# One Trainium2 core: self-attention's decay multiply and row maximum fused, FP4 rounding of FFN weights split between VectorE and GpSimd, masked queries made inside the loop

## The reference

```
x = x + cross_attention(layernorm(x), ctx)     # 16 heads of 64
x = x + self_attention(layernorm(x))           # 16 heads of 16, latent keys and values
x = x + ffn(layernorm(x))                      # FP4 rounded inputs and weights, width 704

# self_attention, for each batch and head
scores = q @ k_rec.T / sqrt(256)
scores = scores * decay                        # decay[i, j] = exp(-0.01 * |i - j|)
out    = softmax(scores) @ v_rec

# rounding of the last dimension in blocks of 16
scale = max(|block|) / 6;  q = nearest_fp4(block / scale) * scale
```

## Time and profile before

| | |
|---|---|
| median of 3 runs | 1395.5 us (1392.56 to 1398.28) |
| the profiled execution's own time | 1398.23 us |
| its span in the trace | 1396.5 us |
| mean granted clock of TensorE | 0.973 |
| PE busy | 1314.0 us (94%) |
| DVE busy | 1001.9 us (72%) |
| ACT busy | 870.6 us (62%) |
| POOL busy | 669.5 us (48%), none of it from 1200.4 us on |
| attention loop | first scores at 1219.58 us, last values end at 1320.03 us |

### The profile page before, as it was taken

The page is one execution under the profiler, slowest core; times in us unless marked ns, Lnnn a source line. Parts: engine busy times, 40 slices in busy tenths (PEclk is TensorE's granted clock), DMA queues, the critical chain, the costliest instruction groups (busy, mean ns, idle before and its releaser), DMA issues. The chain is left out here.

```text
span 1396.5 us, 24647 instructions
## 1 busy us (share of the span) xinstructions
PE 1314.0 (94%) x9280; PEld 1123.8 (80%) x9280; DVE 1001.9 (72%) x1382; ACT 870.6 (62%) x1704; POOL 669.5 (48%) x817
## 2 busy tenths in 40 slices
PE   5899999999999999999999999999999998689857
PEld 5788888888888888888888888888888887378734
DVE  3666678667876777678866886688668868489576
ACT  3667666666666766666666666666666666346511
POOL 5654755475546544565547554755475444000000
PEclk9999999999999999999999999999999999889878
DMA  4010000000000011100000000000000003000000
GB/s 128 16 38 13 16 1 9 8 16 1 9 9 31 1 39 31 39 31 1 9 17 8 1 9 8 16 1 9 9 1 1 1 8 99 0 1 1 1 0 15
DMA packets 24902, 22.95 MB, mean 16 GB/s; under 512 B 4433, under 2 KB 24529, under 8 KB 24785
## 3 DMA queue, kind: packets, MB, share of 16 engines
q1 hardware_dynamic: 24784, 21.38, 5.1%
HBM read 20.85 MB, written 0.52 MB: 15 GB/s over the span
## 5 line engine op out<-in xcount | busy, mean ns | idle before, releaser
L661 ACT ACTIVATE pT_hi<-psT 128x512 fp32r<-128x512 f32 x512 | 292.4, 601 | 238.2 <-PE psT L417 223.5
L752 DVE TENSOR_TENSOR pT_lo<-psT,pT_hi 128x512 fp32r<-128x512 f32 x512 | 330.3, 685 | 101.0 <-ACT pT_hi L661 100.5
L746 DVE TENSOR_REDUCE negm<-psS 128x1 f32<-128x1024 f32 x256 | 311.8, 1218 | 47.9 <-PE psS L407 47.9
L325 POOL TENSOR_TENSOR kT<-kraw,khi 64x512 fp32r<-64x512 f32 x252 | 324.8, 1289 | 0.0
L626 ACT ACTIVATE prob<-psS,negm 128x1024 f32<-128x1024 f32 x256 | 285.8, 1116 | 1.0 <-DVE negm L746 1.0
L319 POOL CAST khi<-kraw 128x512 fp32r<-128x512 f32 x126 | 76.9, 610 | 415.6 <-ACT kraw L636 414.2
L417 PE MATMUL psT<-ident,prob 128*128 128x128 f32 x2048 | 268.5, 274 | 2.1 <-DVE pT_lo L752 2.1
L433 PE MATMUL psO<-pT_hi,v 128*128 128x256 f32 x1024 | 267.5, 294 | 2.1 <-DVE pT_lo L752 1.8
L417 PEld LDWEIGHTS psT<-ident,prob 128*128 128x128 f32 x2048 | 233.2, 140 | 36.1 <-issue 10.3
L434 PE MATMUL psO<-pT_lo,v 128*128 128x256 f32 x1024 | 255.7, 282 | 0.0
L433 PEld LDWEIGHTS psO<-pT_hi,v 128*128 128x128 f32 x1024 | 195.4, 191 | 3.3 <-DVE pT_lo L752 3.1
(11 more groups left out here) (231 smaller groups left out, 1578.6 us busy)
## 6 DMA issues: line engine op xcount, KB each, us to landing
cst<-in_ctx_dram SPq DMA_DIRECT2D x12, 512.0 KB, 3.8
oT<-in_ctx_dram SPq DMA_DIRECT2D x4, 512.0 KB, 5.3
wraw<-in_L_xattn_Wk_dram SPq DMA_DIRECT2D x8, 256.0 KB, 2.7
wraw<-in_L_xattn_Wv_dram SPq DMA_DIRECT2D x8, 256.0 KB, 2.7
wraw<-in_L_xattn_Wq_dram SPq DMA_DIRECT2D x8, 256.0 KB, 2.7
wo<-in_L_xattn_Wo_dram SPq DMA_DIRECT2D x8, 256.0 KB, 2.7
ff_wdn<-in_L_ffn_w_down_dram SPq DMA_DIRECT2D x1, 704.0 KB, 7.5
ff_win<-in_L_ffn_w_gate_dram SPq DMA_DIRECT2D x1, 640.0 KB, 5.0
```

The lines of the kernel that those rows point to most:

```text
L325: pool.tensor_tensor(kT[half, m // 2 % KRING, h, 1, :], raw[own, :], khi[own, :].bitcast(F32), ALU.subtract).then_inc(k_split, 1)
L661: act.activation(pT_hi[:, i % PRING, :], psT[:, t % 2, :], ACT.Copy).then_inc(ph_ok, 1)
L746: dve.tensor_reduce(negm[:, g % 2, h, qt, c:c + 1], psS[:, qt, :], AX.X, ALU.max, negate=True)\
L752: dve.tensor_tensor(pT_lo[:, i % PRING, :], psT[:, t % 2, :], pT_hi[:, i % PRING, :].bitcast(F32), ALU.subtract).then_inc(pl_ok, 1)
```

## The change

1. The multiply and the maximum of a unit become two `tensor_tensor_reduce` of 128x256, one for each half, that write the product to `sa_s` and the row maximum to a new tile `sa_top`; a TENSOR_SCALAR of 128x2 then turns its sign into `negm`. PE's wait for the PSUM tile is on `top_ok`, behind the pair.
2. Operations 4, 7, 8 and 9 of each weight chunk move to POOL. The tiles `wa`, `wm`, `wamax` and `wrs` get two buffers. The six operations left on DVE stand behind a unit's sign turn: operation 0 at unit `CHUNK_AT[c]`, 1 to 3 one unit later, 5 and 6 three units later. DVE's operation 5 waits for POOL's operation 4; DVE's operation 0 of chunk c waits for POOL's last of chunk c - 2. `turn_w` is at iterations `CHUNK_AT[c]` + 8 and + 9.
3. The first 3 masked queries are made ahead of the loop, the other 13 one at a time behind the sign turn of units 0 to 12.
4. The tiles of the row rounding are slices of the weight tiles, and DVE waits for POOL's last weight operation before the LayerNorm of the FFN.

```diff
-    WPU = 2
+    CHUNK_AT = (0, 4, 9, 13, 18, 22)
...
+        top = tile("sa_top", [P, U, QT])
...
-        wa = tile("ff_wa", [P, WCH])
+        wa = tile("ff_wa", [P, 2, WCH])
...
+            for c in range(CHUNKS):
+                src = weight_rows(c)
...
+                a, m = wa[:, c % 2, 0:width], wm[:, c % 2, 0:width]
+                pool.wait_ge(wq, 6 * c + 4)
+                pool.tensor_tensor(blocks(a), blocks(src), wide(wrs), ALU.mult).then_inc(wp, 1)
+                pool.wait_ge(wq, 6 * c + 6)
+                pool.tensor_tensor(a, a, m, ALU.add).then_inc(wp, 1)
+                pool.wait_ge(wp, 4 * c + 2)
+                pool.tensor_tensor(a, a, m, ALU.subtract).then_inc(wp, 1)
+                pool.wait_ge(wp, 4 * c + 3)
+                pool.tensor_tensor(blocks(src), blocks(a), wide(wamax), ALU.mult).then_inc(wp, 1)
...
-                    pe.wait_ge(sd_done, u - 1)
+                    pe.wait_ge(top_ok, 2 * (u - 1))
...
-                pe.wait_ge(wq, quantized_at(c))
+                pe.wait_ge(wp, 4 * (c + 1))
...
-            for h in range(H):
+            def own_rows(h):
                 dve.wait_ge(proj_ok, at[("q", h // HPT)] + 1)
                 dve.tensor_scalar(qm[:, h, :], qT[:, h // HPT, :], hm[:, h % HPT:h % HPT + 1], None, ALU.mult)\
                    .then_inc(qm_ok, 1)
+            for h in range(3):
+                own_rows(h)
...
-                dve.tensor_tensor(sd_[:, u % 2, :, :], psS[:, u % 2, :, :], decay[:, :, :], ALU.mult)\
-                   .then_inc(sd_done, 1)
-                dve.wait_ge(sd_done, u + 1)
-                dve.tensor_reduce(negm[:, u, :], sd_[:, u % 2, :, :], AX.X, ALU.max, negate=True)\
-                   .then_inc(max_ok, 1)
+                for qt in range(QT):
+                    dve.tensor_tensor_reduce(sd_[:, u % 2, qt, :], psS[:, u % 2, qt, :], decay[:, qt, :], 1.0, -3.0e38,
+                                             ALU.mult, ALU.max, top[:, u, qt:qt + 1]).then_inc(top_ok, 1)
+                dve.wait_ge(top_ok, 2 * u + 2)
+                dve.tensor_scalar(negm[:, u, :], top[:, u, :], -1.0, None, ALU.mult).then_inc(max_ok, 1)
+                if u + 3 < H:
+                    own_rows(u + 3)
+                for c in range(CHUNKS):
+                    if u == CHUNK_AT[c]:
+                        weight_op(c, 0)
+                    elif u == CHUNK_AT[c] + 1:
+                        for op in (1, 2, 3):
+                            weight_op(c, op)
+                    elif u == CHUNK_AT[c] + 3:
+                        for op in (5, 6):
+                            weight_op(c, op)
...
+            dve.wait_ge(wp, 4 * CHUNKS)
             normalize(0)
```

More of the change, by code:

```diff
@@ L975, in self_attention_and_ffn @@
         wdT = tile("ff_wdT", [P, FT, D])
-        wa = tile("ff_wa", [P, WCH])
-        wm = tile("ff_wm", [P, WCH])
-        wamax = tile("ff_wamax", [P, WCH // BLOCK])
-        wrs = tile("ff_wrs", [P, WCH // BLOCK])
+        wa = tile("ff_wa", [P, 2, WCH])
+        wm = tile("ff_wm", [P, 2, WCH])
+        wamax = tile("ff_wamax", [P, 2, WCH // BLOCK])
+        wrs = tile("ff_wrs", [P, 2, WCH // BLOCK])
         xnf = tile("ff_xn", [P, R, D])
@@ L985, in self_attention_and_ffn @@
         res = tile("ff_res", [P, R, D])
-        fa = tile("ff_a", [P, F])
-        fm = tile("ff_m", [P, F])
-        famax = tile("ff_amax", [P, F // BLOCK])
+        fa, fm, famax, frs = wa[:, 0, 0:F], wm[:, 0, 0:F], wamax[:, 0, 0:F // BLOCK], wrs[:, 0, 0:F // BLOCK]
         spare = tile("ff_spare", [P, 1])
-        frs = tile("ff_rs", [P, F // BLOCK])
         psG = psT[:, :, :, :].rearrange("p a b c -> p (a b c)")
@@ L994, in self_attention_and_ffn @@
         psD = psO
-        wq, wt_ps, wt_ok = sem("ff_wq"), sem("ff_wt_ps"), sem("ff_wt_ok")
+        wq, wp, wt_ps, wt_ok = sem("ff_wq"), sem("ff_wp"), sem("ff_wt_ps"), sem("ff_wt_ok")
         fstat_ok, fsd_ok, fxn_ok = sem("ff_stat"), sem("ff_sdok"), sem("ff_xnok")
@@ L1004, in self_attention_and_ffn @@
         proj_ps, proj_ok = sem("sa_proj_ps"), sem("sa_proj_ok")
-        qm_ok = sem("sa_qm_ok")
-        s_ok, sd_done, max_ok, exp_ok = sem("sa_s_ok"), sem("sa_sd"), sem("sa_max"), sem("sa_exp")
+        qm_ok, top_ok = sem("sa_qm_ok"), sem("sa_top_ok")
+        s_ok, max_ok, exp_ok = sem("sa_s_ok"), sem("sa_max"), sem("sa_exp")
         t_ok, pT_ok, av_ok = sem("sa_t"), sem("sa_pTok"), sem("sa_av")
@@ L1017, in weight_rows @@
             return wdn[:, c - 4, :]
-        def quantized_at(c):
-            return OPS * (c + 1)
         def turns_at(i):
             for c in range(CHUNKS):
-                if i in (5 * c + 7, 5 * c + 8):
-                    return 2 * c + i - (5 * c + 7)
+                if i in (CHUNK_AT[c] + 8, CHUNK_AT[c] + 9):
+                    return 2 * c + i - (CHUNK_AT[c] + 8)
             return None
@@ L1040, in _ @@
             pool.memset(epst[:, :], EPS).then_inc(eps_ok, 1)
+            blocks = lambda t: t.rearrange("p (n k) -> p n k", k=BLOCK)
+            for c in range(CHUNKS):
+                src = weight_rows(c)
+                width = src.shape[1]
+                nb = width // BLOCK
+                wide = lambda t: t[:, c % 2, 0:nb].unsqueeze(2).to_broadcast([P, nb, BLOCK])
+                a, m = wa[:, c % 2, 0:width], wm[:, c % 2, 0:width]
[7 more added lines that the diff above has]
+                pool.tensor_tensor(blocks(src), blocks(a), wide(wamax), ALU.mult).then_inc(wp, 1)
         @block.tensor
@@ L1369, in quantize, with weight_op @@
                     dve.tensor_tensor(blocks(src), blocks(a), wide(amax), ALU.mult).then_inc(done, 1)
[L1371 to L1381, removed]
+            def weight_op(c, op):
+                if op == 0 and c % 2 == 0:
+                    dve.wait_ge((wg_in, wu_in, wd_in)[c // 2], 16 if c == 4 else 32)
+                if op == 0 and c >= 2:
+                    dve.wait_ge(wp, 4 * (c - 1))
+                elif op == 5:
+                    dve.wait_ge(wp, 4 * c + 1)
+                elif op > 0:
+                    dve.wait_ge(wq, 6 * c + min(op, 5))
+                i = c % 2
+                quantize(op, weight_rows(c), wa[:, i, :], wm[:, i, :], wamax[:, i, :], wrs[:, i, :], wq)
             for u in range(U):
-                for i in range(WPU * u, min(WPU * u + WPU, CHUNKS * OPS)):
-                    weight_op(i)
                 dve.wait_ge(s_ok, u + 1)
```

## The result

The changed kernel takes 1389.2 us (median of 12 runs, 1385.5 to 1392.1) against 1397.0 before; the ratio is 0.9948, 95% interval 0.9935 to 0.9961, so **7 us or 0.5% faster**. The forecast was 1397, inside a range of 1385 to 1406, and within 0.5%. The time lies in the range, but the sign is wrong: I forecast no difference, with a sum of +1.2 us, and there is a gain.

A forecast was written before the change was run, and what follows sets the result against it. The prediction took DVE to bound the loop, PE close behind. Loop +3.3 us (collisions 8.6 less 5.3 of room), start -1.0, tail -1.1 gave +1.2 us; laid on the median of 1395.5, 1397 us, range 1385 to 1406.

The forecast's parts named there:

- the collisions: Loop of 32 units: POOL's work shuts out DVE's sign turns and masked queries, +8.6 us (bounds 0 and 10.7 + 0.8).
- the room in the loop: Scores(7) to scores(31), 24 units: 65.9 us against 60.6 of PE work, so at most 5.3 us to give back.
- the start and the tail: Loop's two ends: values(0) 1.0 us earlier; less DVE work and two weight turns fewer at the end, 1.1 us.
- DVE sets the pace: Loop before the change: DVE, busy 59.9 of 66 us, bounds it at 2.75 us a unit, PE close behind.
- the ring: Loop: scores, DVE, exponentials, copy, values, back to scores; 4.62 us per two units against PE's 4.68, no slack.
- PE's floor: PE in the loop: 2.34 us for a unit without waits, plus 0.40 for a weight turn.
- The fused pair: DVE in each unit: 0.42 us per fused instruction, 0.84 a pair; a unit takes 1.07 where it took 1.41.
- Rival 3: DVE in the loop: fused instruction no faster than the two replaced, pair 1.40 us; about 1399 us, chance 0.07.
- rival 1: Loop: the sign turn of 2 columns isn't shut out by POOL, 8.2 us less: 1387 us, chance 0.28.
- the walk through a chunk: Loop, chunk at unit c: sign turn waits 0.7 us at c + 2, 0.9 at c + 4; 1.3 a chunk after cover.
- The pile-up: DVE: masked query behind operation 8 (2.4 us), operation 1 behind operation 9 (0.9 each); 4.2 us in all, half counted.
- Rival 2: Loop: gaps in PE's work make its clock fall again; 1403 us with one fall, 1409 with two; chance 0.20.

The follow-up runs named there:

- before_copy_first: The kernel before with ACT's copy of unit u - 2 put ahead of the exponentials of unit u, nothing else; 1384.4 us, ratio 0.9901.
- fused_only: The kernel before with only the fused pair and the sign turn; weight operations stay on DVE, all masked queries ahead of the loop; 1384.1 us, ratio 0.9928.
- copy_first_reduce: The changed kernel with ACT's copy ahead of the exponentials and the sign turn made by a TENSOR_REDUCE; 1377.0 us, ratio 0.9855.
- no_pool_work: The changed kernel with POOL's four weight operations per chunk left out, small memsets carrying the semaphores; 1382.1 us, ratio 0.9899.
- copy_first: The changed kernel with ACT's copy of unit u - 2 ahead of the exponentials of unit u; 1377.7 us, ratio 0.9863.
- changed_again: The changed kernel unaltered, measured a second time on another chip; 1386.9 us, ratio 0.9942.

## Why the prediction was wrong

The step that failed is the price of the collisions, 8.6 us "paid by PE nearly in full", where the runs show 3.3. The other terms were also too low, by less: the room in the loop, 5.3 us where 6.6 were there to be had, the start and the tail. By the traces the span fell by 8.6 us (1396.5 to 1387.9) where the sum had it rise by 1.2: loop -3.3 for +3.3, start -2.0 for -1.0, tail -2.6 for -1.1, and 0.8 outside the loop, for which there was no term and no run gives a cause.

**The bound before: wrong.** "DVE sets the pace" rested on 59.9 busy us of 66 and on a chain that runs through DVE's weight operations. before_copy_first takes 5.0 us off the stretch with DVE's work untouched, so DVE had that much slack. I had described the ring correctly a paragraph later, but used it only to price late results, and not to ask whether it was already the bound.

**PE's floor: wrong, 2.34 for 2.20.** This is the first number of the sum that failed; the turns' 0.40 was close (0.32 and 0.61, 0.43 on average). The row I took had no idle time noted in front of its matmuls, but the waits of the kernel before, from 1246.7 to 1310.2 us (total, times, longest), show where it can hide:

```profile
PEld saO L1127 <- ACT sa_pT L1284: 8.0, 16, 1.0
PE saO L1127 <- ACT sa_pT L1284: 4.4, 9, 0.7
```

The weight loads of values waited for the copy 16 times, its matmuls only 9 times by the rows. A values group of 0.81 without a wait is 0.91 with one at its first weight load (and behind a long weight turn, wait or none). With the floor of 55.3 the room in the 23 units is 63.4 - 55.3 = 8.1 us. "Can give back 5.3 us, and no more" is refuted by fused_only (6.7) and copy_first_reduce (7.8); before_copy_first gets 5.0 of it without any saving.

**The fused pair: right.** 0.42 for 0.42, 1.0 us a unit for 1.07. Rival 3 is out.

**The collisions: right in kind, 8.6 us for 3.3.** They are there, at the places named, and the sign turn of 128x2 is shut out, so rival 1 is out; rival 1's 1387 us came near by luck, for a reason that isn't so. Of the walk through a chunk, unit c + 2 was late by 0.1 to 0.8 for 0.7, unit c + 4 by 0.5 to 0.65 for 0.9 (in the chunk at 18 not at all). Operation 4 took 1.50 on POOL, where I had 1.84. In the stretch 12 sign turns were late, by 7.2 us together; no_pool_work shows that PE paid 3.3 of them. "Paid by PE nearly in full" was the error. Where the rest went can be read unit by unit, from the starts of scores in the changed kernel and in no_pool_work; a late sign turn of unit u reaches PE first in its iteration u + 1, through the copy of unit u - 2. Unit 11's was 0.60 late, and iteration 12, which has a long weight turn, took 2.81 us in both: hidden. Unit 14's was 1.21 late and cost 0.96 (3.47 us for 2.51): paid for the greater part. Unit 15's, right behind it, was 0.76 late and cost 0.19 (2.39 for 2.20): in the shadow of the one before. The prediction had both kinds of cover, at 0.3 a chunk and for one unit in three, and gave them too little. copy_first, where twelve late sign turns of 7.9 us in sum leave the stretch 1.0 above copy_first_reduce, shows that it is a matter of slack. The pile-up of operation 1 behind operation 9 didn't come; twice, at 1262.2 and 1295.9, the sign turn itself met the start of operation 9 and was 1.2 us late. The pile-up of a masked query behind operation 8 came once, 2.12 us at unit 4, in the half-clock stretch, where PE doesn't wait for it.

**Start and tail: 1.0 and 1.1 for 2.0 and 2.6.** values(0) came 1.7 us earlier, for 1.0. For the tail the difference is the clock: it stayed at 1.00 to the end of the loop in this execution. In changed_again it did not, and the tail took 9.5 us, 0.4 below before's; the start there gained only 0.3. So what both gave in the first trace isn't the change's alone, and the part that depends on the clock is luck.

**Rival 2: did not come to pass** in the changed kernel's long stretch (PEclk 1.00).

By the prediction's own steps: the loop came to -3.3 where the sum said +3.3. Of these 6.6 us, 5.3 are collisions that were not paid, and the other 1.3 are room that the floor had denied (6.6 for 5.3: before's 63.4 less no_pool_work's 56.8).

**Still open:** what decides in a single execution whether PE's clock falls behind 1230 us. fused_only shows the size of it. Its six executions are four of 1383.4 to 1384.3 us at a mean clock of 0.979 and two of 1389.0 to 1389.3 at 0.973. In the traces the fall is absent where values(0) came within 8.2 us of scores(0), and present from 8.5 us on, but each is one execution. I did not vary it by itself.

## What to carry to other kernels

Take an engine's floor from a unit with no wait anywhere around it, weight loads too, and check it against a second unit; the smallest repeat found counts, not a typical one, and each kind of unit needs its own (here plain, with a short weight turn, with a long one). An instruction that comes late costs only what the consumer has no slack for: follow each one to the unit that waits for it. Before an engine that is 90% busy is called the bound, look for a cheap reordering that takes its results off the path: here two swapped blocks on ACT gave almost twice the gain of the whole change. Work handed to GpSimd can shut out small VectorE instructions on the path; a form that isn't shut out, such as a reduce over one element in place of a multiply by -1, costs nothing and gave back 2.8 us.

## What the runs showed of the hardware that I had not expected

- A 128x2 TENSOR_SCALAR takes 0.17 us alone and up to 1.39 beside POOL, ending as POOL's instruction does; a 128x2 TENSOR_REDUCE in its place took 0.155 us each of 32 times, beside the same work on POOL.
- POOL's two-input operation on 128x768 mostly takes 1.50 us with a broadcast block value as second input and 1.81 with two full tiles.
- Either engine can be the one that is held up. A masked query at 1247.21, 0.14 us ahead of POOL's next operation, ran at its normal 0.47, and POOL's took 2.02 in place of 1.81 us; one at 1231.15, 0.02 ahead of POOL's by the rows, took 2.12 in place of 0.48, and POOL's its normal 1.82. What decides between them at such distances two cases don't show.
- A weight turn whose last transpose has 64 rows in place of 128 lengthens PE's unit by 0.61 us, where one with three full transposes adds 0.32.
- The fused instruction's accumulator read (0.08 us) is a row of its own, and delays nothing. The Trainium skill (VectorE: DVE Perf Modes, "Two Vector instructions with no wait between them") counts such an operation as two instructions, and the trace shows the two.
